# Mamba and expert layer on one core: x's statistics move from VectorE to ScalarE, one product from GpSimd to VectorE, and ScalarE's blocks of jobs are cut and reordered

## The reference

```
h   = layernorm(x)
x   = x + (h + mamba(h))
      mamba: xn = rmsnorm(h) * rms_w;  xs, res = split(xn @ W_in)          # 512 + 512
             xs = silu(causal conv of 4 taps(xs) + conv_b)
             dt, B, C = split(xs @ W_x)                                    # 512, 16, 16
             dt = softplus(dt @ W_dt);  A = -exp(A_log)                    # A: 512 x 16
             s_t = exp(A dt_t) * s_(t-1) + dt_t B_t xs_t;  y_t = sum over 16 states of s_t C_t
             result: (y * silu(res)) @ W_out
h   = layernorm(x)                                                         # tokens 512 e .. 512 e + 511 go to expert e
out = x + (silu(h @ w1[e]) * (h @ w3[e])) @ w2[e]                          # 256 -> 704 -> 256
```

## Time and profile before

| | before |
|---|---|
| time, median of 3 runs | 985.3 us (985.3 to 986.16) |
| the profiled execution: its time, its span | 985.27 us, 983.5 us |
| PE, DVE, POOL, ACT busy in the span | 913.5, 900.4, 892.1, 732.3 us |
| span of a steady iteration | 113.19 us |
| mean granted TensorE clock | 0.983 of full |

### The profile page before, as it was taken

The page is one execution under the profiler, slowest core; times in us unless marked ns, Lnnn a source line. Parts: engine busy times, 40 slices in busy tenths (PEclk is TensorE's granted clock), DMA queues, the critical chain, the costliest instruction groups (busy, mean ns, idle before and its releaser), DMA issues.

```text
span 983.5 us, 13018 instructions
## 1 busy us (share of the span) xinstructions
PE 913.5 (93%) x4172; PEld 594.7 (60%) x4172; DVE 900.4 (92%) x966; ACT 732.3 (74%) x1305; POOL 892.1 (91%) x425
## 2 busy tenths in 40 slices
PE   6989989999999999999999999999999998769898
PEld 4545455655765576755856566754766556745765
DVE  5889899899999999999999999999999989999951
ACT  4667877978778878888779877888788785567630
POOL 1498899999999999999999999999999999999920
PEclk9999999999999999999999999999999999779899
DMA  5580154012642049021651038120580027200110
GB/s 175 222 298 22 43 215 173 29 40 100 260 157 67 1 171 343 4 68 59 233 225 43 25 103 340 76 68 12 190 315 21 27 95 277 102 22 3 59 50 21
DMA packets 43476, 116.82 MB, mean 119 GB/s; under 512 B 8592, under 2 KB 27024, under 8 KB 34192
## 3 DMA queue, kind: packets, MB, share of 16 engines
q1 hardware_dynamic: 41552, 115.94, 32.2%
q10 hardware_dynamic: 1856, 0.04, 0.1%
HBM read 110.21 MB, written 5.77 MB: 118 GB/s over the span
## 4 chain that ended last, share of the span: by engine, by line
PE 36%; DVE 36%; ACT 15%; issue 11%; DMA 1%; POOL 0%; DVEq 0%; SPq 0%; ACTq 0%; POOLq 0%
DVE ring L658 25%; PE gbank L1091 19%; DVE ring L643 9%; PE ybank L1154 7%; PE gbank L1105 6%; ACT ebank L787 4%; ACT hb L1020 2%; ACT sres L868 1%; ACT xs L864 1%; ACT L1016 1%; PE gbank L1099 1%; ACT L876 1%; ACT L872 1%; DMA hb<-in_L_attn_W_x_dram 1%; PE gbank L1225 1%
## 5 line engine op out<-in xcount | busy, mean ns | idle before, releaser
L658 DVE TENSOR_TENSOR_SCAN ring<-ebank,state,ring 128x512 f32<-128x512 f32 x512 | 623.7, 1267 | 28.8 <-ACT ebank L787 21.6
L516 POOL TENSOR_TENSOR hc<-ring,c_all 128x1024 f32<-128x1024 f32 x255 | 600.8, 2381 | 14.0 <-DVE ring L658 6.4
L787 ACT ACTIVATE ebank<-dt_,a_neg 128x512 f32<-128x512 f32 x512 | 347.2, 689 | 165.0 <-DVE ring L658 162.5
L1154 PEld LDWEIGHTS ybank<-ident,hc 128*128 128x128 f32 x2048 | 237.8, 144 | 106.5 <-issue 52.0
L1154 PE MATMUL ybank<-ident,hc 128*128 128x128 f32 x2048 | 265.2, 278 | 31.9 <-POOL hc L516 23.2
L502 POOL TENSOR_TENSOR ring<-b_all,u 128x1024 f32<-128x1024 f32 x109 | 259.5, 2381 | 9.9 <-DVE taken L607 9.5
L643 DVE TENSOR_TENSOR ring<-b_all,ubank 128x1024 f32<-128x1024 f32 x145 | 173.4, 1196 | 0.0
L1091 PE MATMUL gbank<-xT,w 128*128 128x512 f32 x320 | 148.1, 597 | 15.2 <-DVE hb L738 12.4
L1091 PE MATMUL gbank<-xT,w_a 128*128 128x512 f32 x256 | 119.1, 602 | 8.3 <-DVE dt_ L632 4.4
L1091 PEld LDWEIGHTS gbank<-xT,w 128*128 128x128 f32 x320 | 57.3, 190 | 82.2 <-issue 56.7
L1091 PE MATMUL gbank<-xs,w_a 128*128 128x512 f32 x224 | 100.8, 593 | 0.7 <-ACT sres L805 0.7
(11 more groups left out here) (146 smaller groups left out, 750.9 us busy)
## 6 DMA issues: line engine op xcount, KB each, us to landing
b_all<-bc_kept SPq DMA_DIRECT2D x32, 1024.0 KB, 6.7
c_all<-bc_kept SPq DMA_DIRECT2D x32, 1024.0 KB, 8.4
w<-in_L_ffn_w_dram SPq DMA_DIRECT2D x16, 640.0 KB, 4.9
w_a<-in_L_attn_W_in_dram SPq DMA_DIRECT2D x7, 1024.0 KB, 4.9
w_a<-wc_kept SPq DMA_DIRECT2D x7, 1024.0 KB, 4.8
w2s<-in_L_ffn_w_dram SPq DMA_DIRECT2D x8, 640.0 KB, 9.4
xin<-in_L_attn_x_dram SPq DMA_DIRECT2D x9, 512.0 KB, 3.6
x<-in_L_attn_x_dram SPq DMA_DIRECT2D x7, 512.0 KB, 6.4
```

Of the source, the lines that this page charges most:

```text
L516: ch_ok.by(e.tensor_tensor(hc[:, q % HC, :, :], ring[:, q % RING, :, :], c_all[:, n:n + NG, :], ALU.mult))
L658: h_ok.by(e.tensor_tensor_scan(row, ebank[j % 2][:, :], row, initial=state[:, q, n:n + 1], op0=ALU.mult, op1=ALU.add))
L787: e_ok.by(e.activation(ebank[j % 2][:, :], dt_[:, d, :], ACT.Exp, scale=a_neg[:, d, k:k + 1]))
L1154: last = e.matmul(ybank[:, cols(b)], hc[:, q % HC, n, cols(b)], ident[:, :], is_transpose=True, start=(k == 0 and n == 0 and b == 0), stop ...
```

## The change

ScalarE now makes the mean and the variance of x: `x_sums` copies each of the four blocks of rows (128x256) with an accumulator, `x_mean` turns the sums into minus the mean, and `x_squares` squares x minus the mean with an accumulator. The copies go into the tile `u`, as a scratch. Chunks 0 and 1 still use `x_stats` on DVE. The product B times u of tile 21 is made on DVE, not on POOL (13 tiles for POOL, not 14). DVE's `gated(1)` comes at tile 20, `hidden(2)` to `hidden(4)` one tile earlier. On ACT, `res_silu` comes behind the silus of the gate, `rooted` at tile 24, `before_conv` and `normal` are spread over more tiles. POOL's `front` comes at tile 24. The table PLAN and PE's tables stay.

```diff
-    POOL_BU = (1, 4, 7, 10, 11, 14, 17, 18, 21, 22, 23, 24, 27, 29)
+    POOL_BU = (1, 4, 7, 10, 11, 14, 17, 18, 22, 23, 24, 27, 29)
...
+        sums = Event("sums", NT)
...
-            table = [(4, "scan", u_of(ND - 1)), (10, "back", back), (21, "next", front), (24, "front", u_of(0)),
+            table = [(4, "scan", u_of(ND - 1)), (10, "back", back), (24, "next", front), (24, "front", u_of(0)),
...
-            table0 = [(3, "late", u_of(1)), (7, "late", u_of(2)), (10, "late", u_of(3)), (23, "next", front),
+            table0 = [(3, "late", u_of(1)), (7, "late", u_of(2)), (10, "late", u_of(3)), (26, "next", front),
...
-                     (19, "next", x_stats), (19, "scan", gated(1)), (20, "back", hidden(0)), (20, "back", hidden(1)),
-                     (20, "back", hidden_tail), (21, "back", hidden(2)), (22, "back", hidden(3)), (23, "back", hidden(4)),
+                     (20, "scan", gated(1)), (20, "back", hidden(0)), (20, "back", hidden(1)),
+                     (20, "back", hidden_tail), (20, "back", hidden(2)), (21, "back", hidden(3)), (22, "back", hidden(4)),
...
-                      (19, "next", x_stats), (19, "scan", gated(0)), (23, "scan", gated(1)), (27, "front", dt_of(0)),
+                      (19, "scan", gated(0)), (23, "scan", gated(1)), (27, "front", dt_of(0)),
...
+            def x_sums(*bs):
+                def job(c, i):
+                    x_in.wait(e, c)
+                    bup_ok.wait(e, i, before(pool_bu(i), 2 * GPD))
+                    for b in bs:
+                        sums.by(e.activation(u[:, b // 2, b % 2 * D:(b % 2 + 1) * D], xin[:, b, :], ACT.Copy, accum_out=mv[:, b, 0:1]))
+                return job
+
+            def x_mean(c, i):
+                sums.wait(e, c - 2)
+                x1a_ok.wait(e, c - 3)
+                roots.by(e.activation(st[:, c % 3, 2, :], mv[:, :, 0], ACT.Copy, scale=-1.0 / D))
+
+            def x_squares(*bs):
+                def job(c, i):
+                    roots.wait(e, c, 1)
+                    for b in bs:
+                        last = e.activation(u[:, b // 2, b % 2 * D:(b % 2 + 1) * D], xin[:, b, :], ACT.Square, bias=st[:, c % 3, 2, b:b + 1], accum_out=mv[:, b, 1:2])
+                    if NT - 1 in bs:
+                        stats.by(last)
+                return job
...
-                roots.by(e.activation(mine[:, 0, :], mv[:, :, 1], ACT.Ln, scale=1.0 + EPS, bias=eps2))
-                roots.by(e.activation(mine[:, 1, :], mv[:, :, 1], ACT.Ln, bias=eps))
-                roots.by(e.activation(mine[:, 2, :], mv[:, :, 0], ACT.Copy, scale=-1.0))
-                roots.wait(e, c, 2)
+                of = 1.0 if c < 2 else 1.0 / D
+                roots.by(e.activation(mine[:, 0, :], mv[:, :, 1], ACT.Ln, scale=(1.0 + EPS) * of, bias=eps2))
+                roots.by(e.activation(mine[:, 1, :], mv[:, :, 1], ACT.Ln, scale=of, bias=eps))
+                if c < 2:
+                    roots.by(e.activation(mine[:, 2, :], mv[:, :, 0], ACT.Copy, scale=-1.0))
+                roots.wait(e, c, 3)
...
-            def normal(c, i):
-                scales.wait(e, c)
-                for b in range(NT):
-                    xn_ok.by(e.activation(xin[:, b, :], xin[:, b, :], ACT.Identity,
-                                          bias=st[:, c % 3, 3, b:b + 1], scale=st[:, c % 3, 4, b:b + 1]))
+            def normal_rows(*bs):
+                def job(c, i):
+                    scales.wait(e, c)
+                    for b in bs:
+                        xn_ok.by(e.activation(xin[:, b, :], xin[:, b, :], ACT.Identity,
+                                              bias=st[:, c % 3, 3, b:b + 1], scale=st[:, c % 3, 4, b:b + 1]))
+                return job
...
                 e.preload_act_table(ACT.Silu)
-                if has_front(i):
-                    res_silu(c + 2, i)
                 wait_read(e, i, "GATE", FT - 1)
                 silu_ok.by(e.activation(hb[:, 0:FT, :], hb[:, 0:FT, :], ACT.Silu))
                 silu_ok.wait(e, c, 1)
                 silu_ok.by(e.activation(hb[FR:P, FT, :], hb[FR:P, FT, :], ACT.Silu))
+                if has_front(i):
+                    res_silu(c + 2, i)
                 e.preload_act_table_set(LOG_EXP)
...
-            table = [(0, "front", before_conv(0, 1)), (2, "front", before_conv(2, 3)), (2, "back", y_read(ND - 1)),
-                     (3, "front", convolved(0)), (4, "front", convolved(1)), (5, "front", convolved(2)), (5, "back", residual(0, 1)),
+            table = [(0, "front", before_conv(0)), (1, "front", before_conv(1)), (2, "front", before_conv(2)), (2, "back", y_read(ND - 1)),
+                     (3, "front", before_conv(3)), (3, "front", convolved(0)), (4, "front", convolved(1)), (5, "front", convolved(2)), (5, "back", residual(0, 1)),
...
-                     (13, "front", bc_read), (14, "back", turned("OXT")), (16, "front", softplus(0)), (17, "back", gate(0, 1)),
+                     (13, "front", bc_read), (14, "back", turned("OXT")), (16, "front", softplus(0)), (17, "back", gate(0, 1)), (17, "next", x_sums(0, 1)),
...
-                     (20, "back", gate_silus), (22, "next", rooted), (24, "front", softplus(1)), (25, "front", softplus(2)),
-                     (26, "ahead y", y_read(2)), (27, "scan y", y_read(2)), (29, "next", normal), (30, "front", softplus(ND - 1)),
+                     (20, "back", gate_silus), (21, "next", x_sums(2, 3)), (21, "next", x_mean), (22, "next", x_squares(0, 1)),
+                     (23, "next", x_squares(2, 3)), (24, "next", rooted), (24, "front", softplus(1)), (25, "front", softplus(2)),
+                     (26, "ahead y", y_read(2)), (27, "scan y", y_read(2)), (28, "next", normal_rows(0, 1)), (29, "next", normal_rows(2, 3)), (30, "front", softplus(ND - 1)),
...
-                      (19, "front", silus_first), (20, "scan", y_read(1)), (20, "front", res(0, 1)), (22, "front", res(2, 3)),
-                      (24, "front", bc_read), (25, "next", rooted), (25, "front", softplus(0)), (27, "front", softplus(1)),
+                      (19, "front", silus_first), (20, "scan", y_read(1)), (20, "front", res(0, 1)), (22, "front", res(2, 3)), (23, "next", x_sums(0, 1)),
+                      (24, "front", bc_read), (24, "next", x_sums(2, 3)), (25, "next", x_mean), (25, "next", x_squares(0, 1)), (26, "next", x_squares(2, 3)),
+                      (26, "next", rooted), (25, "front", softplus(0)), (27, "front", softplus(1)),
```

More of the change, by code:

```diff
@@ L819, in rooted @@
                 roots.by(e.activation(mine[:, 5, :], mine[:, 7, :], ACT.Identity, bias=1.0))
-            def normal(c, i):
-                scales.wait(e, c)
-                for b in range(NT):
-                    xn_ok.by(e.activation(xin[:, b, :], xin[:, b, :], ACT.Identity,
-                                          bias=st[:, c % 3, 3, b:b + 1], scale=st[:, c % 3, 4, b:b + 1]))
+            def normal_rows(*bs):
[5 more added lines that the diff above has]
+                return job
+            normal = normal_rows(*range(NT))
             def turned(name):
```

## The result

The changed kernel takes 987.73 us (median; 987.19 to 988.44) beside 986.01 us for the kernel before, measured in the same rounds (985.08 to 987.32). The ratio is 1.0019, 95% interval 1.001 to 1.0027: slower by 0.19%, where 981.5 us and a gain were forecast. The time lies inside the forecast's range (975.5 to 989), on the other side of the old kernel's.

What follows compares the result with a forecast made beforehand. Bound: a chain of waits over PE for half an iteration, DVE and ACT otherwise. Per iteration 0 + 0.6 - 0.46 + 0.15 - 0.9 = -0.6 us, five times -3.0; first iteration -0.3, last chunk -0.5: -3.8, so 981.5 us, range 975.5 to 989.

Steps and rivals of the forecast that it cites:

- Tiles 21 to 25: ACT's sums, mean, squares and moved `rooted`: tile 25's first scan +0.6 us an iteration, bounds -0.2 and +2.2.
- What PE gains is slack: Silu block at tile 21: UP 2 goes nearly 1.3 us earlier, without gain, since DVE is late next.
- a gain on PE alone is soon lost: Tile 31: PE's path meets ACT and DVE's almost at one time; PE waited only 0.23 us for xT.
- I take all 0.9: Tiles 0 to 3, `before_conv` one at a time: tile 1's stall goes, 0.9 us gained an iteration (0.5 to 0.9).
- The block is as long as before: Silu block with `res_silu` behind the gate silus: same instructions, same length, and it sets tile 21.
- Cost here 0: First sums at tile 17: a 0.5 us stall before tile 18, but the table load starts where it did.
- S = 1.3 and Q = 1.5: Upper costs in us of an accumulating pair on ACT: S for Copies (taken as 0.9), Q for Squares (1.05).
- the term of -0.5: Last chunk: DVE reaches tile 24 at 914.2 instead of 914.72; 0.5 us gained, bounds 0 and 2.3.
- The accumulators are dear: Rival, chance 0.18: ACT's accumulating jobs, tiles 21 to 25, at upper bounds cost +1.5 us an iteration, 992 us.
- Square needs another table: Rival, chance 0.03: four extra ACT table loads of 1.28 us at tiles 22 and 23, five times, about 1007 us.
- PE is the real bound: Rival, chance 0.13: earlier UP 2 and tile 1's stall count in full, 1.3 + 0.9 or more six times, 972 us.
- Gains and stalls cancel: Rival, chance 0.20: POOL and DVE relief lies under the block, S, Q near 1.1 and 1.25; within 2 us of 985.3.

Runs made afterwards that it cites:

- p21_on_pool: The changed kernel with the product of tile 21 back on POOL: 986.94 us, ratio 1.0006 to the kernel before.
- stats_on_dve: The changed kernel with x's statistics back on DVE at tile 19, the rest as changed: 993.25 us, ratio 1.007 to the kernel before.
- both_moves: The changed kernel with the first sums at tile 19 and `rooted` at tile 25: 983.42 us, ratio 0.9968 to the kernel before.
- conv_split_alone: The kernel before with only `before_conv` split, one at a time at tiles 0 to 3: 981.24 us, ratio 0.9958 to the kernel before.
- moves_hidden_old: moves_p21_pool with hidden(2) to hidden(4) back at tiles 21 to 23: 983.71 us, ratio 0.9979 to the kernel before.
- moves_p21_pool: both_moves with the product of tile 21 back on POOL: 983.73 us, ratio 0.9975 to the kernel before.
- conv_in_pairs: The changed kernel with `before_conv` in pairs again, at tiles 0 and 2: 991.98 us, ratio 1.0055 to the kernel before.
- rooted_at_25: The changed kernel with `rooted` at tile 25, behind softplus(1) and `down_on(0)`: 985.71 us, ratio 0.9991 to the kernel before.
- sums_at_19: The changed kernel with the first pair of sums at tile 19 instead of 17: 986.35 us, ratio 1.0004 to the kernel before.

## Why the prediction was wrong

**The steps that held.** The accumulators: 0.80 and 0.98 us a pair, for 0.9 and 1.05. Tiles 21 to 25: from tile 21's scan to tile 25's it was 12.45 us and is 471.19 - 458.08 = 13.11, so +0.66 for +0.6. The stalls at tiles 30 and 1 went. POOL's relief gave nothing (p21_on_pool has the same period). The statistics alone were not tried on the old kernel, so "hidden by the block" for them is left untried; stats_on_dve shows only that they don't fit beside product 21.

**The step that failed** is that PE has slack ("What PE gains is slack", "a gain on PE alone is soon lost"), and with it "I take all 0.9" for `before_conv`. The forecast added all its terms along DVE: a delay at tiles 21 to 25, then gains at tiles 30 and 1. It had asked what PE gains in this change and never what it loses. But the delay passes to PE at tile 27, through `y_read(2)`, a copy of 0.6 us that stands on ACT behind exps that wait for DVE, and the two gains come only after that. PE carries the delay on unchanged, 34.5 us long, to CV 2, and tile 6 waits for CV 2. PE had 0.77 us of air on this path, and tile 25 was 0.9 late: 0.66 from tiles 21 to 25, which the forecast had (0.6), and 0.23 at tile 21, which it had at nothing ("The block is as long as before", "Cost here 0"). At tile 5 the forecast's gain was there (0.53 us); at tile 6 it had turned into a loss of 0.13. Even the forecast's own 0.6 would have left 113.19 - 0.77 + 0.6 = 113.02 on this path (an estimate), and not 112.59.

The runs price the parts of a steady iteration. The kernel after has 113.32. Take from it `rooted` at tile 25 (0.55, since it stood before tile 25's exp), the first sums away from tile 17 (0.13) and `y_read(2)` a tile earlier (0.28), and 112.36 is left; measured with all three, and product 21 back on POOL, 112.37. The split alone gives 112.40. So the rest of the change is worth nothing even where it is best placed here, and costs 0.92 us an iteration where it was placed. With `y_read(2)` left in its place it still costs 0.23 (both_moves, 112.63). What the accumulating jobs alone cost, no run separates from their placement.

**Smaller misses.** The first sums at tile 17 were costed at 0: the stall of 0.3 to 0.65 us at tile 18 was foreseen, but 0.13 of it reaches the period. "The block is as long as before (same instructions)" was short by 0.14 us, since an overlap between neighbours hung on their order. UP 2 goes 1.1 us earlier in the ordinary iterations, for "nearly 1.3". The first iteration was to give 0.3; from its table load of tile 19 to the next one of tile 8 it was 76.24 us and is 76.21, and in conv_split_alone 76.18, so of the 0.62 expected from the split 0.06 is there. The forecast's upper bound for tiles 21 to 25 (+2.2) doesn't follow from its own figures, S = 1.3 and Q = 1.5, which add 1.3 to the 0.6 and make +1.9; nothing measured hangs on it.

**The last chunk** was to give 0.5 us. I measured it at tile 24's scan: from the load of the gate block it was 16.16 us and is about 16.0, so even there it is 0.2 for 0.5. And the end doesn't hang there. The chain of waits of the kernel after, last chunk:

```profile
914.35 2.38 DVE ring L659 x2
...
917.38 0.19 ACT state L792
917.57 0.50 ACT gbank L1024
...
918.20 5.46 PE gbank L1136 x12
```

It goes from tile 23's scans over the state copy to `down_on(0)` and PE's DOWN. The wait for POOL that I removed, at tile 24, lay beside this path; product 21 and one hidden job more, which went ahead of tile 23's scans, lie on it. DOWN starts 16.26 us behind the load with neither (before, moves_hidden_old), 16.94 with the hidden job alone (moves_p21_pool, p21_on_pool) and 17.52 with both. As long as POOL has product 21, POOL's products set how soon PE gets on behind DOWN (it waits 0.70 us for them at 926.33 before), and the stretch is 52.82 to 52.89 in all those kernels, whatever DOWN's start and clock. Without it that cushion is gone: the stretch is 52.54 to 52.58 where DOWN takes 4.47 to 4.51, 53.27 where it takes 5.22, and 53.60 to 53.93 where it runs at half clock to its end (5.46). So the term of -0.5 comes out between -0.3 and +1.0, and its missing part is TensorE's clock, which the forecast left out although DOWN ran at half clock in this chunk before the change too. PE is idle for 3.79 us ahead of it now, and was for 0.68 before.

**The rivals.** "The accumulators are dear" is out by their rows. "Square needs another table" is out. "PE is the real bound" had the right engine, but it priced an earlier UP 2, which ends in PE's wait for `y_read(2)`: I let PE only gain. "Gains and stalls cancel" is nearest to the outcome, but for other reasons than it named. What stays open is why the second period is 113.66. It has 0.35 more of a stall before tile 18, also in conv_in_pairs and rooted_at_25 and not in sums_at_19 or p21_on_pool; the exp of tile 18 came no later in it (at 441.51, 33.08 us behind the load, for 33.08 and 33.09 in its neighbours), so something else held DVE. Open too are what sets the moment at which the clock is back, and what the scatter of the start comes from.

## What to carry to other kernels

When jobs are added to an engine with idle time, list every job on it that another engine waits for in that stretch, down to the half-microsecond ones, and price its delay along that engine's own path, not only along the path that is longest now. Gains that come on the first path behind the hand-over don't help the second. The length of a new wait doesn't say what it costs: here the wait of 0.97 us was free and the one of 0.79 behind it set the period, because the second job came no earlier when the first wait went. To find the one that counts, look in several variants for a place from which the distance to the end stays the same. A removed wait counts only if the chain of the end runs over it; so a gain or a delay must be followed until the next place where the paths meet (here five tiles into the next iteration), not to the place where the stall was. And try the parts one at a time: one line of this change was worth 4 to 5 us, and was hidden by the rest.

## What the hardware showed that was not expected

Reading ACT's accumulator is a separate instruction of 0.19 us (128x1). It overlaps both neighbours by about 0.1 us: from Copy to Copy it is 0.40 us (440.71 to 441.11) for a Copy of 0.41, which without the read would overlap its neighbour and step by some 0.31. So a read adds about 0.09 (an estimate from these rows), for the 0.14 that I took.

Two long ACTIVATEs overlapped by 0.10 us in one order (128x2048 first, then 128x2560) and not at all in the other (128x2560, 64x512, 128x2048), in the same table set. Between the first two of these the kernel has a semaphore wait, in both orders; between 64x512 and 128x2048 it has none on ACT's own work. Why they don't overlap was not tried.

The same program, with the same waits in its last chunk, ran its 12 matmuls of DOWN 0 in 4.47 or 5.46 us, by the granted clock after the same idle time; 1.3 us of the kernel's end depend on it. In the steady iterations of this kernel the clock stood at 1.00; in two iterations each of stats_on_dve and res_silu_first it fell to half at UP 2, and 12 matmuls of 128x512 took 7.11 us for 5.42. There the profile shows PE waiting 1.91 to 2.29 us just before, and other iterations of the same kernels with a wait of 1.91 to 1.94 kept the full clock.
